# Attention scores for the row maximum: 32-row operands in four row groups of the array, and one-piece transfers per head

## What is computed

```python
x = x + 0.5 * _L0_ffn_ref(_layernorm(x), router_w, router_b, w1, b1, w2, b2)
x = x + _L0_attn_ref(_layernorm(x), w_qkv, w_proj, b_proj)
x = x + 0.5 * _L0_ffn_ref(_layernorm(x), router_w, router_b, w1, b1, w2, b2)

# _L0_attn_ref, B=4, L=1024, H=16, Dh=8
qkv = (x @ w_qkv).reshape(B, L, 3, H, Dh)
attn = jnp.einsum('bhid,bhjd->bhij', q, k) * scale
attn = attn + phi_bias(L)[None, None]     # log(exp(-|pos_i - pos_j|) + 1e-8), pos = i*PHI % 1
attn = jax.nn.softmax(attn, axis=-1)
out = jnp.einsum('bhij,bhjd->bhid', attn, v)
out @ w_proj + b_proj
```

## Time and profile before

| | |
|---|---|
| median of 3 runs | 1227.99 us |
| lowest, highest | 1227.91, 1228.85 us |
| span of the profiled execution | 1235.2 us |
| attention (from DVE's first row to the last store of sums) | 272.7 to 1018.9 us |

### The profile page before, as it was taken

One profiled execution on the slowest core, in us unless ns is written; L12 is line 12 of the kernel. 1 busy time (PEld: TensorE's weight loads), 2 busy tenths in 40 slices (PEclk: granted clock), 3 DMA queues, 4 the chain that ended last, 5 costly groups with the idle time before them and its releaser, 6 DMA issues. The chain is left out here.

```text
span 1235.2 us, 26880 instructions
## 1 busy us (share of the span) xinstructions
PE 1084.3 (88%) x6562; PEld 529.4 (43%) x6563; DVE 933.5 (76%) x1753; ACT 708.5 (57%) x1574; POOL 419.9 (34%) x628
## 2 busy tenths in 40 slices
PE   5549993759999999999999999999999986729997
PEld 4449993422222222222222222222222216629997
DVE  6447774869888888888888888888888817837885
ACT  1024441444777777777777777777777761104443
POOL 2524343443223332323232333323232322642433
PEclk9999997787999999999999999999999996659999
DMA  9221113240111111111111111111111146432221
GB/s 329 97 55 44 41 43 88 96 148 20 30 34 37 32 31 34 36 31 32 35 35 31 31 36 33 31 33 36 32 31 35 28 103 202 164 109 69 67 67 30
DMA packets 54063, 77.03 MB, mean 62 GB/s; under 512 B 15679, under 2 KB 35269, under 8 KB 53368
## 3 DMA queue, kind: packets, MB, share of 16 engines
q1 hardware_dynamic: 48264, 65.25, 18.0%
q0 software_dynamic: 5056, 10.53, 2.3%
q10 hardware_dynamic: 704, 0.79, 0.3%
HBM read 54.61 MB, written 25.41 MB: 65 GB/s over the span
## 5 line engine op out<-in xcount | busy, mean ns | idle before, releaser
L946 DVE TENSOR_REDUCE nmax<-psS 128x1 f32<-128x1024 f32 x512 | 602.9, 1220 | 109.2 <-PE psS L899 109.1
L960 ACT ACTIVATE prob<-psE 128x512 f32<-128x512 f32 x1024 | 537.1, 606 | 179.2 <-PE psE L891 178.9
L899 PE MATMUL psS<-kop,qop 120*128 120x512 bf16 x1024 | 393.8, 388 | 11.6 <-DVE mpart L930 8.6
L891 PE MATMUL psE<-qop,kop 123*128 123x512 bf16 x1024 | 389.1, 382 | 3.4 <-ACT prob L960 2.6
L1004 POOL TENSOR_TENSOR prob<-prob,const 128x512 f32<-128x512 f32 x128 | 162.4, 1269 | 472.5 <-ACT prob L960 472.5
L915 PE MATMUL psV<-prob,vst 128*9 128x512 f32 x2048 | 267.1, 595 | 1.0 <-issue 0.8
L891 PEld LDWEIGHTS psE<-qop,kop 123*128 123x128 bf16 x1024 | 99.3, 98 | 314.1 <-ACT prob L960 219.0
L899 PEld LDWEIGHTS psS<-kop,qop 120*128 120x128 bf16 x1024 | 99.5, 98 | 117.7 <-DVE nmax L946 17.7
L752 ACT ACTIVATE siga<-psGa,w1sa 128x128 f32<-128x128 f32 x156 | 44.5, 368 | 62.9 <-PE psGa L660 62.9
L752 ACT ACTIVATE sigb<-psGb,w1sb 128x128 f32<-128x128 f32 x156 | 44.5, 368 | 60.7 <-PE psGb L660 60.7
L915 PEld LDWEIGHTS psV<-prob,vst 128*9 128x9 f32 x2048 | 30.8, 88 | 109.9 <-issue 109.9
(11 more groups left out here) (163 smaller groups left out, 1023.2 us busy)
## 6 DMA issues: line engine op xcount, KB each, us to landing
qop<-qk_parts SPq DMA_DIRECT2D x192, 48.0 KB
kop<-qk_parts SPq DMA_DIRECT2D x192, 48.0 KB
qk_parts<-part_attend SPq DMA_DIRECT2D x16, 384.0 KB, 2.8
xsb<-sorted_b SPq DMA_DIRECT2D x39, 128.5 KB
weighted_sums<-osum SPq DMA_DIRECT2D x256, 18.0 KB
w1a<-in_w SPq DMA_DIRECT2D x1, 4128.0 KB
w1b<-in_w SPq DMA_DIRECT2D x1, 4128.0 KB
qop<-mrow SPq DMA_DIRECT2D x256, 1.5 KB
```

Source lines behind the costliest of these rows:

```text
L891: nc.tensor.matmul(psE[BANK[n]][:], kop[b][0:TROWS, kt * P:(kt + 1) * P], qop[b][0:TROWS, cols], start=True, stop=True).then_inc(s_t, 1)
L899: last = nc.tensor.matmul(psS[kt % 2][:, half, :], qop[b][0:SROWS, kt * P:(kt + 1) * P], kop[b][0:SROWS, cols], start=True, stop=True)
L946: nc.vector.tensor_reduce(nmax[r % 2][:, qt:qt + 1], psS[qt % 2][:], AX.XY, ALU.max, negate=True).then_inc(s_max, 1)
L960: nc.scalar.activation(prob[r % 2][:, lo:lo + HALF], psE[BANK[n]][:], ACT.Exp).then_inc(s_exp, 1)
```

## The change

What it does:

- `psS` no longer holds the bias. Its operands are the new tiles `qS` and `kS` of 4 x 32 rows, four copies of the same 32 rows of q (parts h, h, m, l) and of k (h, m, l, h). A score matmul reads 32 rows; the two halves of a query tile and its neighbour tile go to four different row groups of the array (L911). So the number that is subtracted is the row maximum of q.k alone, without the bias; it is then carried in two bf16 parts, not three (POOL has two operations where it had four, `psE` has 122 rows).
- PE's order within a quarter of a head is: two `psE`, four `psS`, two `psE`, four `psV`.
- In the attend phase q is stored five times and k six times, in the order `QSEQ` and `KSEQ`, so that each operand of a head is one run of rows in DRAM; 11 DMAs a group where there were two.
- `load_head` is four DMAs, of 256, 256, 144 and 144 KB, with row counts 4 x 32, 4 x 32, 3 x 24, 3 x 24; it was six of 48 KB.
- The sums of a head are stored as all 128 rows of `osum` in one DMA of 256 KB; `load_sums` has eight DMAs a batch where it had four, to other places of `num` and `den`.

```diff
@@ phase_tokens, attend, SP
-                    for z in range(2):
+                    for z, (to, seq) in enumerate(((d.q, QSEQ), (d.k, KSEQ))):
                         sp.wait_ge(s_part, 2 * n + z + 1)
-                        sp.dma_start(d.qk[z, :, b * P:(b + 1) * P, c].rearrange("a p t -> p a t"),
-                                     part[:, n % 2, z, :, :]).then_inc(s_out[n % 2], 16)
+                        for at, a in enumerate(seq):
+                            sp.dma_start(to[b * HEADS:(b + 1) * HEADS, at, :, c],
+                                         part[:, n % 2, z, "hml".index(a), :]).then_inc(s_out[n % 2], 16)
@@ load_head
-    rows = bass.ds(head * DH, DH)
-    for a in range(3):
-        at = slice(a * 3 * DH, (a + 1) * 3 * DH)
-        sp.dma_start(g.qop[b][at, :], d.qk[0, a, rows, :].unsqueeze(0).to_broadcast([3, DH, L])
-                     ).then_inc(g.s_op[b], 16)
-        sp.dma_start(g.kop[b][at, :], d.qk[1, :, rows, :]).then_inc(g.s_op[b], 16)
+    def rows(src, at, parts, repeat, step):
+        size = len(QSEQ if src is d.q else KSEQ) * DH * L
+        return bass.AP(tensor=src.tensor, offset=head * size + at * DH * L,
+                       ap=[[step * DH * L, repeat], [L, parts * DH], [1, L]])
+
+    sp.dma_start(g.qS[b][:], rows(d.q, 0, 4, 4, 0)).then_inc(g.s_op[b], 16)
+    sp.dma_start(g.kS[b][:], rows(d.k, 2, 4, 4, 0)).then_inc(g.s_op[b], 16)
+    sp.dma_start(g.qop[b][0:COMBO, :], rows(d.q, 2, 3, 3, 0)).then_inc(g.s_op[b], 16)
+    sp.dma_start(g.kop[b][0:COMBO, :], rows(d.k, 0, 3, 3, 1)).then_inc(g.s_op[b], 16)
@@ load_sums
-    for a in range(2):
-        sp.dma_start(g.den[:, b % 2, a, :], sums[b, a, :, DH, :].rearrange("h (j q) -> h j q", q=P))\
-            .then_inc(g.s_den_in[b], 16)
-        sp.dma_start(g.num[:, b % 2, a, :], sums[b, a, :, 0:DH, :]).then_inc(g.s_num_in[b], 16)
+    for j in range(4):
+        a, half = j // 2, j % 2
+        sp.dma_start(g.den[half * 64:half * 64 + 64, b % 2, a, :],
+                     sums[b, j, :, DH, :].rearrange("h (j q) -> h j q", q=P)).then_inc(g.s_den_in[b], 16)
+        sp.dma_start(g.num[:, b % 2, a, half * HALF:(half + 1) * HALF], sums[b, j, :, 0:DH, :])\
+            .then_inc(g.s_num_in[b], 16)
@@ phase_attention, SP
-                    for j in range(4):
-                        sp.dma_start(d.sums[bass.ds(i - 2, 1), j // 2, :,
-                                            (j % 2) * HALF:(j % 2 + 1) * HALF].squeeze(),
-                                     osum[r % 2][32 * j:32 * j + VW, :]).then_inc(s_os[r % 2], 16)
+                    sp.dma_start(d.sums[bass.ds(i - 2, 1), :, :].squeeze(),
+                                 osum[r % 2][:]).then_inc(s_os[r % 2], 16)
@@ phase_attention, PE
+                def score(qt):
...
+                    if later(at, 2, 1) or qt >= 2:
+                        pe.wait_ge(s_max, 8 * (i + 2) + qt - 1)
+                    for half in range(2):
+                        lo = 32 * (qt % 2 * 2 + half)
+                        last = nc.tensor.matmul(psS[qt % 2][:, half, :],
+                                                qS[b][lo:lo + SROWS, qt * P:(qt + 1) * P],
+                                                kS[b][lo:lo + SROWS, half * HALF:(half + 1) * HALF],
+                                                start=True, stop=True)
+                    last.then_inc(s_s, 1)
...
+                for p in range(4):
+                    if live(at, 0):
+                        weigh(2 * p)
+                    if live(at, 2):
+                        score(2 * p)
+                        score(2 * p + 1)
+                    if live(at, 0):
+                        weigh(2 * p + 1)
+                    if live(at, -1):
+                        gather(p)
@@ phase_attention, POOL
-                    nc.gpsimd.tensor_tensor(res[:], nm[:], mp[:, 0, :], ALU.subtract)
-                    pool.drain()
-                    nc.gpsimd.tensor_copy(mp[:, 1, :], res[:])
-                    pool.drain()
-                    nc.gpsimd.tensor_tensor(mp[:, 2, :], res[:], mp[:, 1, :], ALU.subtract).then_inc(s_mp, 1)
+                    nc.gpsimd.tensor_tensor(mp[:, 1, :], nm[:], mp[:, 0, :], ALU.subtract).then_inc(s_mp, 1)
```

More of the change, by code:

```diff
@@ L34 @@
 MAX0 = BIAS0 + BIASN
-SROWS = MAX0
-TROWS = MAX0 + 3
+TROWS = MAX0 + 2
+QSEQ, KSEQ = "lhhml", "hmlhmh"
+STORES = len(QSEQ) + len(KSEQ)
+SROWS = 4 * DH
 PBLK = L + P
@@ L880, in step, with weigh @@
             def step(i, r, at, q):
-                for kt in range(KT):
+                def weigh(kt):
+                    b = r % NBUF
                     for half in range(2):
[L883 to L910, removed]
-                            pe.wait_ge(s_diag, 2 * i - 1 + kt // 4)
-                            pe.wait_ge(s_exp, 16 * i - 8 + 8 * (kt // 4))
-                        for j in range(4):
-                            k, half = kt - 1 + j // 2, j % 2
-                            last = nc.tensor.matmul(
-                                psV[32 * j:32 * j + VW, :], vst[(r + 1) % 2][:, k, :],
-                                prob[(r + 1) % 2][:, k * PBLK + half * HALF:k * PBLK + (half + 1) * HALF],
-                                start=(kt == 1), stop=(kt == 7))
-                        if kt == 7:
-                            last.then_inc(s_pv, 1)
@@ new lines, in weigh @@
+                        n = 2 * kt + half
+                        if n == 0:
+                            pe.wait_ge(s_mr[b], 64 * filled(q, r, 0))
+                        if later(at, 0, 1) or n >= BANK_AGE[n]:
+                            pe.wait_ge(s_exp, 16 * i + n + 1 - BANK_AGE[n])
+                        nc.tensor.matmul(psE[BANK[n]][:], kop[b][0:TROWS, kt * P:(kt + 1) * P],
+                                         qop[b][0:TROWS, half * HALF:(half + 1) * HALF],
+                                         start=True, stop=True).then_inc(s_t, 1)
@@ new lines, in gather @@
+                def gather(p):
+                    if p == 0:
+                        pe.wait_ge(s_vst, i)
+                        if later(at, -1, 1):
+                            pe.wait_ge(s_ev, i - 1)
+                    if p in (0, 2):
+                        pe.wait_ge(s_diag, 2 * i - 1 + p // 2)
+                        pe.wait_ge(s_exp, 16 * i - 8 + 8 * (p // 2))
+                    for j in range(4):
+                        k, half = 2 * p + j // 2, j % 2
+                        last = nc.tensor.matmul(
+                            psV[32 * j:32 * j + VW, :], vst[(r + 1) % 2][:, k, :],
+                            prob[(r + 1) % 2][:, k * PBLK + half * HALF:k * PBLK + (half + 1) * HALF],
+                            start=(p == 0), stop=(p == 3))
+                    if p == 3:
+                        last.then_inc(s_pv, 1)
```

42 lines of the change are left out of this document (24 added, 18 removed).

## The result

| | before | after |
|---|---|---|
| median of 4 runs, us | 1228.42 (1227.91 to 1229.41) | 1280.36 (1267.66 to 1285.62) |
| span of the profiled execution | 1235.2 | 1265.4 |
| first store of q, k to DVE's memset of psV | 224.73 to 272.70, 48.0 | 214.59 to 284.86, 70.3 |
| 48 heads in the middle of the loop, each | 11.31 | 11.67 |

The changed kernel takes 1.0416 times as long, with a 95% interval of 1.0358 to 1.0475. The forecast was 1215 with a range of 1195 to 1255: the sign is wrong, and the time lies outside the range. The profiled run of after took 1267.66, 12.7 under the median. The profiled run of before is one whose expert stage ahead of the loop takes 10 longer than in after (first store at 224.73 and 214.59); nothing there was changed. So the stretches are compared, not the spans.

The account below looks back on a forecast made before the run. PE was taken to set the period, 11.3 us a head, DVE 15% behind. Loop -31, stage +19, ends -1.3 and +0.5 make -13: span 1222, less 7 gives 1215 us, range 1195 to 1255.

Parts of the forecast that it names:

- PE's work a head: Attention loop: PE alone would need 2.50 us a quarter, 10.0 a head; the head was taken as 10.8 instead of 11.3.
- the cycle of PE and DVE: Attention loop: PE and DVE hold each other through the two score tiles, 2.64 us a quarter, 10.6 a head.
- Four row groups: Scores on PE: four products on four row groups take 0.54 us a quarter with stagger and both switches, instead of 0.87.
- The rate of the DMA engines: Loop transfers: first three engines carry 229,000 bytes a head at 24 GB/s, 9.5 us, plus sums 0.7: 10.2 of 10.8.
- The cover of the maxima: Loop: row maxima land about 12 us after a head's first load, needed at 12.6, leaving 0.6.
- Rival 1: Loop: three DMA engines become the bound; at 21 GB/s a head takes 11.5, total 1258 us; chance 0.19.
- the sign turn at 11.0 a head: Loop: from 11.0 us a head the change stops being faster, as 62 x 0.3 = 19.
- 62 heads: Loop total: 62 x (11.3 - 10.8) = -31 us.
- The stage: Stage writing q and k: 88 stores instead of 16, at 0.64 us each on SP's queue, cost +19 us.
- The ends: After the loop: one store of the last sums instead of four, -1.3 us; reloading sums with 32 DMAs, +0.5.
- The 7 that the prediction took off: Whole run: profiled execution before took 1235.2 us, median 1227.99; the same 7 came off span 1222.

Follow-up runs that it names:

- the first experiment: Changed kernel with a head's loads as 14 DMAs of one block of rows each instead of 4, same bytes: 1212.69 us, ratio 0.9881 to before.
- the last experiment: The changed kernel run once more, unmodified, in a second session on another chip for a second profile: 1286.3 us, ratio 1.0421 to before.

## Why the prediction was wrong

- **PE's work a head: right.** The forecast took 10.8, and the cycle of PE and DVE alone gave 10.6, 2.64 a quarter. The kernel with spread loads has heads of 10.57, and its pairs of quarters (psE at 609.45, 614.75, 620.02) take 5.30 and 5.27 for the 5.28 of the working. The rows in the first experiment show the cycle itself: 2.78 to the end of both reductions, as in the working, and PE held until then. The working added 0.1 for the release, an estimate, and 0.05 for the issue, which no row shows; measured are 0.06 from the end of the reductions (615.55) to the weights (615.61) and 2.38 from there to the first tile of the quarter after (617.99), where 0.05 and W had 2.40.
- **Four row groups: right, slightly dear.** 0.54 forecast for the four with both switches. Measured in after: 0.32 to the next psE with the way out in it, and 0.54 for the two psE before (615.92 to 616.46), 0.11 over their 2 x 0.217: 0.43 in all. The 3 x 0.04 of stagger were the author's estimate; in after the four starts lie within 0.01 (616.46 to 616.47).
- **The rate of the DMA engines: right, the sum a little short.** The working put a load on as many engines as its outermost count, 3 before, 4 and 3 after. The packet records from 430 to 900 fit: of the time in which any 2 KB packet runs, three run at a time for 52% in before, and four for 53% and three for 33% in after. Most 2 KB packets take 84 ns, the 24 GB/s that were taken. Loads and sums run from 684.75 to 695.36, 10.6, where the working had 9.5 + 0.7 = 10.2; in the records the packets around the sums' store take up to 120 ns, and a few at the start 400 and more. The maxima's own packets add 0.26.
- **The cover of the maxima: this step failed**, and it is the miss in the loop. The working had the maxima land "about 12" after a head's first load and be needed at 12.6, a cover of 0.6. Both were wrong. *Needed:* the row at 631.09 in the earlier trace rows isn't the head's first psE but its third; the first stands at 630.20, 0.92 behind the load. In after it is 0.85 (625.64 to 626.49, a head without a wait). So the maxima are needed 10.57 + 0.85 = 11.4 after the first load, not 12.6. *There:* PE is released at 13.4, not 12. The first byte comes 1.43 after the issue instead of 1.0 (0.96 in the first experiment, 1.55 in most heads of before), and the loads and sums take 10.6 instead of 10.2; so they end at 12.0 instead of 11.3. From there to PE's start are another 1.4 (the maxima 0.26, then 1.1 to the release), where the step from 11.3 to 12 had 0.7. The cover is -2.0, not +0.6. As the chain runs over two heads, two heads pay it once: 10.57 + 1.0 = 11.56 a head. The trace of before already held the warning: the last packet of its maxima starts at 628.86; with the 1.1 of after, an estimate, they are usable at 629.96, and PE takes them at 630.20. By that, before had 0.24 to spare.
- **Rival 1 was the right place with the wrong reason.** It gave a head of 11.5 if the engines moved 21 GB/s instead of 24, and a chance of 0.19. The packets moved at 24, and the head took 11.67; that the two are close is luck. The times at both ends of the transfer stand in the same chain as the bytes, and a sum of bandwidth that says 94% full has no place for them. The prediction had the sign turn at 11.0 a head, and the head is above that.
- **62 heads: +22 instead of -31** (62 x 0.36, from the 48 heads). The wait and what goes with it cost 1.1 a head (11.67 against 10.57), 68; heads of 10.57 instead of 10.8 give 14 back.
- **The stage: right, a little short.** +19 forecast, +22.3 measured, at 0.64 a store as taken. The working had SP busy throughout; in after it still rests 0.4 and 1.9 ahead of the second and third group (up to 222.14 and 231.01), which is 2.3 of the 3.3.
- **The ends:** from the last head's first psE to the end of the span are 232.5 before (1002.70 to 1235.2) and 229.9 after (1035.51 to 1265.4), -2.6 where -0.8 was forecast.
- **Sum.** 1215 + 53 (loop) + 3 (stage) - 2 (ends) is 1269, against 1267.66 for the profiled run. The 7 that the prediction took off for the profiled run of before are no part of the change either: that profile's first store, at 224.73, stands where the slower session has it, 8 to 10 later than in the first session's profiles. The median is 12.7 above the profiled run of after; of this I can only say what the last experiment says.

## What to carry over

When a small transfer releases the bound engine, write its chain as a sum of times, each taken from a row: issue to first byte, all bytes that lie ahead of it on its engines, its last packet to the release; and compare that with the time at which it is needed, taken from the first instruction that waits, not from one that looks like it. A share of bandwidth below 1, 10.2 of 10.8 here, didn't answer that question. Merging the DMAs saved time on the issuing queue here: a head's loads are issued in 3.4 in after (683.32 to 686.75) and in 6.3 in the first experiment (608.61 to 614.95). But the merged ones, with outermost counts 4 and 3, moved three or four packets at a time for 85% of the time, and what was issued next waited for them (8.8 from issue to landing for the store of sums, against 2.1): 14 DMAs of the same bytes beat 4 by 5%.

## What the runs showed of the hardware

- Two heads' loads in after start to move 1.4 after the first issue (683.32 to 684.75, 694.76 to 696.20); in most heads of before it is 1.55 and in the first experiment 0.96. PE starts 1.1 after the last packet of the transfer that it waits for (0.9 to 1.2 from the start of that packet in 51 of the 53 heads of after that wait for it).
- Four 32-row products with 512 columns each took 0.32 on four row groups until the next psE started (616.46 to 616.78 in after); in one row group they took 0.97 (603.51 to 604.48 in the kernel with one row group).
- In some heads that follow a wait of 1.3 to 2.7 (two profiles of the changed kernel) PE's granted clock fell to 0.50 for about 3.4, and the 16 psE then spanned 10.2 to 10.7 instead of 9.14. Under the waits of up to 1.2 of the old scores with new transfers it did in no head of the loop; in the kernel with nine stores one of the twelve such heads followed a wait of 1.2.
